# An eight-slot timetable for the way from attention into the feed-forward layer, and attention's scores in two PSUM banks

## What is computed

```python
x = layernorm(x + L0_attn(x))   # 16 heads of 16, q/k/v taken by a plain reshape, causal
x = layernorm(x + L0_ffn(x))    # router: 2 of 8 experts, gelu, all experts computed, gates applied
x = layernorm(x + L1_attn(x))   # 16 query heads of 128 in 4 groups
x = layernorm(x + L1_ffn(x))    # router with capacity 64 per expert
```

## Time and profile before

| what | value |
|---|---|
| median of 3 runs | 963.41 us (960.01 to 964.97) |
| the profiled execution: its own time, its span | 958.42 us, 956.6 us |
| TensorE busy | 862.1 us, 90% of the span |
| VectorE, ScalarE, GpSimd busy | 707.6, 513.9, 388.8 us |
| mean granted TensorE clock | 0.973 |

### The profile page before, as it was taken

How to read it: one execution, slowest core, us unless ns; L and a number is a source line. 1 busy time by engine, 2 the same in 40 slices (tenths; PEclk the granted TensorE clock), 3 DMA queues, 4 the chain that set the end, 5 groups by cost and what they waited for, 6 DMA issues and landing times.

```text
span 956.6 us, 22584 instructions
## 1 busy us (share of the span) xinstructions
PE 862.1 (90%) x8457; PEld 536.4 (56%) x8457; DVE 707.6 (74%) x1953; ACT 513.9 (54%) x1201; POOL 388.8 (41%) x731
## 2 busy tenths in 40 slices
PE   5899888987588888979999999999999999899996
PEld 2455444543344444445665766776676666587654
DVE  3776767676678787559999888888888888632566
ACT  3577667766234444446666555556555555523542
POOL 4445465534345645424343333333332323300285
PEclk7999999999789999999999999999999999999999
DMA  7333322320000000006576655565655655500011
GB/s 261 101 91 90 69 68 57 91 30 7 2 0 2 1 1 1 1 1 123 112 124 115 101 105 94 100 103 98 105 98 97 98 97 103 105 2 1 1 45 45
DMA packets 210428, 65.64 MB, mean 69 GB/s; under 512 B 203008, under 2 KB 206608, under 8 KB 210192
## 3 DMA queue, kind: packets, MB, share of 16 engines
q1 hardware_dynamic: 210320, 64.19, 33.8%
HBM read 17.92 MB, written 4.19 MB: 23 GB/s over the span
## 4 chain that ended last, share of the span: by engine, by line
PE 61%; DVE 12%; issue 10%; POOL 8%; DMA 4%; ACT 3%; SPq 1%; POOLq 0%; DVEq 0%; ACTq 0%
PE bank L418 13%; PE bank L420 12%; PE bank L419 12%; PE bank L545 4%; DMA att<-w_lo 4%; PE bank L769 3%; PE bank L771 3%; PE bank L770 3%; PE bank L466 2%; DVE scr L1215 2%; POOL scr L1727 2%; POOL rstd L1743 2%; DVE w_lo L1265 2%; DVE nm L1241 2%; POOL scr L1732 2%
## 5 line engine op out<-in xcount | busy, mean ns | idle before, releaser
L994 ACT ACTIVATE att<-att,nm 128x512 f32<-128x512 f32 (+3 forms) x256 | 141.5, 553 | 103.7 <-DVE nm L1254 102.3
L418 PE MATMUL bank<-w_hi,scr 128*128 128x256 bf16 (+1 forms) x576 | 173.5, 301 | 13.4 <-DVE scr L1183 12.9
L419 PE MATMUL bank<-w_lo,scr 128*128 128x256 bf16 (+1 forms) x576 | 173.1, 301 | 0.0
L420 PE MATMUL bank<-w_hi,scr 128*128 128x256 bf16 (+1 forms) x576 | 172.9, 300 | 0.0
L904 ACT ACTIVATE scr<-bank 128x256 bf16<-128x256 f32 (+3 forms) x208 | 110.8, 550 | 103.2 <-PE bank L771 41.2
L1241 DVE TENSOR_REDUCE nm<-bank 128x1 f32<-128x512 f32 (+3 forms) x256 | 110.3, 482 | 44.6 <-PE bank L490 42.8
L1254 DVE CUSTOM_DVE_ANT_0 att<-bank,consts 128x512 f32<-128x512 f32 (+3 forms) x256 | 113.3, 483 | 15.0 <-PE bank L420 15.0
L950 ACT ACTIVATE att<-bank 128x512 f32<-128x512 f32 (+1 forms) x192 | 90.9, 529 | 59.8 <-PE bank L529 59.1
L1775 POOL TENSOR_SCALAR wqkv_hi<-att,rr 128x512 bf16<-128x512 f32 (+3 forms) x128 | 65.6, 532 | 138.5 <-DVE rr L1271 138.5
L1775 POOL TENSOR_SCALAR w_hi<-att,rr 128x512 bf16<-128x512 f32 (+3 forms) x128 | 65.6, 532 | 106.5 <-DVE rr L1271 106.5
L1183 DVE TENSOR_TENSOR scr<-bank,scr 128x256 bf16<-128x256 f32 (+1 forms) x144 | 75.8, 536 | 43.1 <-ACT scr L904 43.0
(11 more groups left out here) (180 smaller groups left out, 2038.5 us busy)
## 6 DMA issues: line engine op xcount, KB each, us to landing
scr<-wall_in SPq DMA_DIRECT2D x19, 512.0 KB, 4.9
x_tok<-x_tok_in SPq DMA_DIRECT2D x1, 2048.0 KB, 10.5
v_by_token<-scr SPq DMA_DIRECT2D x16, 128.0 KB, 1.8
scr<-v_by_token SPq DMA_DIRECT2D x16, 128.0 KB, 3.2
scr<-x_t_in SPq DMA_DIRECT2D x3, 512.0 KB, 5.8
out<-x_tok SPq DMA_DIRECT2D x3, 512.0 KB, 2.6
scr<-wqkv_in SPq DMA_DIRECT2D x2, 384.0 KB, 3.4
att<-w_hi SPq DMA_TRANSPOSE x32, 3.3
```

The source lines that it names most:

```text
L418: pe.matmul(out, l_hi, r_hi, start=start, stop=False, skip_group_check=check)
L419: pe.matmul(out, l_hi, r_lo, start=False, stop=False, skip_group_check=check)
L420: return pe.matmul(out, l_lo, r_hi, start=False, stop=stop, skip_group_check=check)
L994: last = act.activation(at, at, ACT.Exp, bias=nm[:, j % 2, qt:qt + 1], scale=-1.0, accum_out=rs[:, j % 2, qt:qt + 1])
```

## The change

- Scores go to banks 0 and 1 alone; head h has bank h, and the hold is one head nearer: `- 1` for `- 2`.
- The V projection and the row of maxima move from bank 7 to bank 2. `l0_values` no longer waits for the K stack's copy but for the copy of the last maxima row (`qt`) and of the last V (`vt`); `l0_row_maxima` waits for `qt`, `vt` and, near the end, for the residual additions `r1` that read bank 2. `l0_stack` drops its waits for `qt` and `vt` and waits for the stack before.
- The steps n = -7 to -1 (seven instead of five) are taken apart and their pieces stand one by one in a table over slots 26 to 33 (`EARLY_AT`); `EARLY` now ends at 0, so that the mixture's step 0 follows slot 33 at once, and the first batch's `logits`, `route`, `choose` and `gate` are in the table too.
- The first six `turn_mix` (`LONE_TURNS`) use bank 7, each after the low part of the one before (`hold(pe, m["tlo"], i)`), and wait for the stacks' copies; the K stack of the last group waits for the two turns before it.
- GpSimd's and ScalarE's loops follow the same table; GpSimd's `add_bias` keeps its place at the ends of slots 27 to 30.
- No arithmetic is added or dropped.

```diff
@@ -67,11 +67,30 @@
-EARLY = range(-LEAD - 2, -2)
-TURNS = [(kind, n + lead) for n in STEPS for kind, lead in TURN_LEADS if 0 <= n + lead < NT]
+EARLY = range(-LEAD - 2, 0)
...
-EARLY_TURNS = sum(0 <= n + lead < NT for n in EARLY for _, lead in TURN_LEADS)
-EARLY_AT = {(NP - 2, 1): 0, (NP - 2, 2): 1, (NP - 1, 0): 2, (NP - 1, 1): 3, (NP - 1, 2): 4}
+EARLY_AT = {
+    (26, 1): (("context", 0),), (26, 2): (("cc", 0),),
+    (27, 0): (("cc", 1),), (27, 2): (("first", 0),),
+    (28, 0): (("join", 0), ("cc", 2)), (28, 1): (("norm", 0),), (28, 2): (("x1", 0), ("first", 1)),
+    (29, 0): (("join", 1), ("cc", 3)), (29, 1): (("norm", 1),), (29, 2): (("x1", 1), ("first", 2)),
+    (30, 0): (("join", 2), ("cc", 4)), (30, 1): (("norm", 2), ("first", 3)),
+    (30, 2): (("join", 3), ("x1", 2), ("cc", 5)),
+    (31, 0): (("norm", 3), ("first", 4)), (31, 1): (("x1", 3), ("join", 4), ("cc", 6)),
+    (31, 2): (("norm", 4), ("logits", 0)),
+    (32, 0): (("x1", 4), ("route", 0)), (32, 1): (("first", 5),), (32, 2): (("join", 5),),
+    (33, 0): (("choose", 0),), (33, 1): (("norm", 5),)}
+def early(p, chunk):
+    return EARLY_AT.get((p, chunk), ())
+TURNS = [(what, t) for at in sorted(EARLY_AT) for what, t in EARLY_AT[at] if what in ("cc", "x1")]
+TURNS += [(kind, n + lead) for n in STEPS[len(EARLY):] for kind, lead in TURN_LEADS if 0 <= n + lead < NT]
+LONE_TURNS = sum(what in ("cc", "x1") for at in EARLY_AT if at < (30, 0) for what, _ in EARLY_AT[at])
+FIRSTS = [at for at in sorted(EARLY_AT) for what, _ in EARLY_AT[at] if what == "first"]
...
@@ -308,7 +327,7 @@
         def turn_bank(i):
-            return i % 2
+            return 7 if i < LONE_TURNS else i % 2
...
@@ -438,9 +457,10 @@
             def l0_values(g):
...
-                hold(pe, a["stk"], g)
+                hold(pe, a["qt"], 2 * g - 3)
+                hold(pe, a["vt"], g)
...
-                    last = mm3(bank[7][:, 0:E], hi, lo, wqkv_hi[:, k, 512:768], wqkv_lo[:, k, 512:768],
+                    last = mm3(bank[2][:, 0:E], hi, lo, wqkv_hi[:, k, 512:768], wqkv_lo[:, k, 512:768],
...
@@ -450,9 +470,10 @@
             def l0_stack(g, which):
...
-                hold(pe, a["qt"], 2 * g - 2 + which)
+                hold(pe, m["tlo"], sum(what in ("cc", "x1") for at in EARLY_AT if at < (2 * g - 4 + which, 1)
+                                       for what, _ in EARLY_AT[at]))
...
-                    pe.wait_ge(a["vt"], g + 1)
+                    hold(pe, a["stk"], g)
...
@@ -474,13 +495,13 @@
-                out = [bank[(6 * p + 2 * chunk + h) % 3] for h in range(2)]
+                out = [bank[h] for h in range(2)]
...
-                                hold(pe, a["max"], 6 * p + 2 * chunk + h - 2)
+                                hold(pe, a["max"], 6 * p + 2 * chunk + h - 1)
...
@@ -496,16 +517,14 @@
             def l0_row_maxima(p):
...
-                if j == 1:
-                    pe.wait_ge(a["vt"], min(g + 3, NT))
-                    pe.wait_ge(a["stk"], min(g + 2, NT))
-                else:
-                    pe.wait_ge(a["stq"], min(g + 2, NT))
+                hold(pe, a["qt"], p)
+                hold(pe, m["r1"], sum(at < (p - 1, 0) for at in FIRSTS))
+                pe.wait_ge(a["vt"], min((p - 3) // 2 + 4, NT))
...
-                pe.matmul(bank[7][:, :], ident_b[:, :], q_stack[g % 2][:, ds(j * TOK, TOK)], start=True, stop=False,
+                pe.matmul(bank[2][:, :], ident_b[:, :], q_stack[g % 2][:, ds(j * TOK, TOK)], start=True, stop=False,
...
-                    last = pe.matmul(bank[7][:, qt * P:(qt + 1) * P], m_cols[p % 2][:, qt, :], ident_b[:, :],
+                    last = pe.matmul(bank[2][:, qt * P:(qt + 1) * P], m_cols[p % 2][:, qt, :], ident_b[:, :],
...
@@ -575,11 +594,21 @@
-                    if (p, chunk) in EARLY_AT:
-                        if EARLY_AT[p, chunk] == 0:
-                            pe.wait_ge(ch_done, 1)
-                            pe.wait_ge(a["max"], 6 * NP)
-                        early_step(EARLY[EARLY_AT[p, chunk]])
+                    for what, t in early(p, chunk):
+                        if what in ("cc", "x1"):
+                            if p < 30:
+                                pe.wait_ge(a["stk"], NT if p > 27 else NT - 1)
+                                pe.wait_ge(a["stq"], NT)
+                            else:
+                                pe.wait_ge(a["max"], 6 * NP)
+                            turn_mix(what, t)
+                        elif what == "first":
+                            if t == 0:
+                                pe.wait_ge(ch_done, 1)
+                            pe.wait_ge(a["qt"], min(p + 2, NP))
+                            first_project(t)
+                        elif what == "logits":
+                            logits(t)
...
             def turn_mix(kind, t):
...
@@ -594,7 +623,7 @@
-                hold(pe, m["tlo"], i - 1)
+                hold(pe, m["tlo"], i if i < LONE_TURNS else i - 1)
...
@@ -973,11 +1001,11 @@
-                    if (p, chunk) in EARLY_AT:
-                        n = EARLY[EARLY_AT[p, chunk]]
-                        if 0 <= n + LEAD:
-                            turned_high("x1", n + LEAD)
-                        turned_high("cc", n + LEAD + 2)
+                    for what, t in early(p, chunk):
+                        if what in ("cc", "x1"):
+                            turned_high(what, t)
+                        elif what == "route":
+                            router_exp(m, 1, TT * NX)
...
@@ -1347,14 +1388,27 @@
-                    if (p, chunk) in EARLY_AT:
-                        n = EARLY[EARLY_AT[p, chunk]]
-                        if n == EARLY[0]:
+                    for what, t in early(p, chunk):
+                        if what == "context":
+                            dve.wait_ge(v_wr, 16 * NT)
...
-                            context(0)
-                        if 0 <= n + LEAD:
-                            norm(n + LEAD, 1)
-                        early_step(n)
+                            context(t)
+                        elif what == "cc":
+                            turned_low(what, t)
+                            context(t + 1)
+                        elif what == "x1":
+                            turned_low(what, t)
+                        elif what == "join":
+                            joined(t, 1)
+                        elif what == "norm":
+                            norm(t, 1)
+                        elif what == "route":
+                            dve.wait_ge(a["pv"], 3 * NT)
+                            route(t)
+                        elif what == "choose":
+                            choose_first(t)
+                            choose_second(t)
+                            gate(t)
...
@@ -1692,8 +1719,11 @@
-                    if (p, chunk) in EARLY_AT:
-                        mix_step(EARLY[EARLY_AT[p, chunk]])
+                    for what, t in early(p, chunk):
+                        if what == "join":
+                            scale_and_shift(t, 1)
+                        elif what == "x1":
+                            add_out_bias(t)
```

More of the change, by code:

```diff
@@ L941, in l0_query_maxima @@
                 act.wait_ge(a["nm"], p + 1)
-                copy(q_max[p % 2], bank[7][:, :]).then_inc(a["qt"], 1)
+                copy(q_max[p % 2], bank[2][:, :]).then_inc(a["qt"], 1)
             def l0_exponentials(p, chunk):
@@ L1240, in l0_maxima @@
                         w = (qt + 1) * P
-                        last = dve.tensor_reduce(nm0[:, p % 2, h, qt:qt + 1], bank[n % 3][:, col:col + w], AX.X,
+                        last = dve.tensor_reduce(nm0[:, p % 2, h, qt:qt + 1], bank[n % 2][:, col:col + w], AX.X,
                                                  ALU.max)
@@ L1327, in sums_inverse, with route, choose_first, choose_second @@
                 dve.wait_ge(m["rc"], half + 1)
-            def early_step(n):
-                if 0 <= n + LEAD:
-                    turned_low("x1", n + LEAD)
-                if 0 <= n + LEAD + 1:
-                    joined(n + LEAD + 1, 1)
-                turned_low("cc", n + LEAD + 2)
-                context(n + LEAD + 3)
+            def route(b):
+                dve.wait_ge(m["lg"], b + 1)
+                tiles_b = slice(b * TT, (b + 1) * TT)
+                dve.tensor_tensor(lg[:, tiles_b, :], bank[2][:, 0:TT * NX].rearrange("p (t x) -> p t x", x=NX),
+                                  rb_bc[:, :].unsqueeze(1).to_broadcast([P, TT, NX]), ALU.add).then_inc(m["lgc"], 1)
+                dve.wait_ge(m["lgc"], b + 1)
+                router_max(dve, chain, lg[:, tiles_b, :], TT, m["lgd"])
+            def choose_first(b):
+                router_first(dve, chain, TT, m["ex"], b + 1)
+            def choose_second(b):
+                router_second(dve, chain, TT)
+            def gate(b):
+                tiles_b = slice(b * TT, (b + 1) * TT)
+                row, wide, top = router_views(TT)
```

(31 more changed lines are left out.)

19 lines of the change are left out of this document (5 added, 14 removed).

## The result

| | before | after |
|---|---|---|
| median of 4 runs | 962.93 us (960.01 to 964.97) | 947.25 us (945.18 to 950.19) |
| the profiled execution, its span | 958.42, 956.6 us | 945.18, 943.4 us |
| mean granted TensorE clock | 0.973 | 0.973 |

The ratio is 0.9853 (95% interval 0.9822 to 0.9884): 1.5% faster, where 1.1% was forecast. Two later sets of runs of the same kernel gave 0.9852 (0.9827 to 0.9877) and 0.9888 (0.9868 to 0.9907). One execution of the kernel with both edits, further down, took 2996 us and is left out of its numbers.

What follows compares the result with a forecast made beforehand. TensorE, busy 90%, was taken as the bound, so gains come from its idle time or low clock. Attention -9.1 and timetable -1.4 gave -10.5 us: 948 against the profiled 958.4, 953 on the median's footing, range 946 to 961.

Steps and rivals of the forecast that it cites:

- The V projection's wait: Steady attention: the V projection no longer waits for VectorE's K-stack copy; -0.90 us in each of 13 pairs of slots.
- The bank cost: Steady attention: with two score banks, scores wait for one more reduction; +0.1 us in odd and +0.1 in even slots.
- Rival (b): Attention pairs: VectorE's reductions set the pace, +0.6 us per pair, 970 us in all; chance 0.06.
- The filling: First attention slots, pipeline filling: the removed 1.4 us wait and three or four bare stalls of 0.4 to 0.6 cancel, 0.
- The timetable: Slot 26 to first experts: slots 26 to 29 +11.3 us, the rest -12.7, sum -1.4; queues on VectorE and GpSimd return the gain.
- the walk: Slot-by-slot count from slot 26 to the first experts, each instruction starting when engine and releasers are ready, at full clock.
- The clock: First experts: low clock after the last stall as before, no difference; a fall from slot 30's stall would cost 1 to 2 us.
- rival (c): Slots 26 to 33: norms caught by GpSimd's big bias additions, 2.0 us each, 959 us in all; chance 0.12.
- (a): Attention: bank stalls eat the gain, -0.1 us per pair, 961 us in all; chance 0.12.
- (e): Attention pair stays at 13.40 us because something else, such as ScalarE's exponentials, takes over; 961 us; chance 0.05.
- Rival (d): Timetable better than walked: biases find GpSimd free, slots 29 and 30 lose 1 us each, not 4; 947 us; chance 0.13.

Runs made afterwards that it cites:

- both edits: Kernel after with attention biases of batches 0 to 3 added in slots 26 and 27, and norm(5) ahead of choose: 941.29 and 942.07 us, ratios 0.9797 and 0.9795.
- the banks alone: Kernel before with only the bank part of the change, turns, biases and early blocks left as they were: 950.44 us, ratio 0.9876.
- the nearer hold: Kernel before with three score banks kept, but each head's scores waiting for one reduction more: 965.47 us, ratio 1.0043.
- the wait put back: Kernel after with the V projection again waiting for the K stack's copy of the group before: 964.32 us, ratio 1.0013.
- the first profile: Kernel after, unchanged, its first profiled execution: 945.18 us, span 943.4 us.
- the second execution: Kernel after, unchanged, profiled a second time: span 949.8 us; its set of runs had a median of 949.61 us.
- the third execution: Kernel after, unchanged, profiled a third time: 60.9 us from the fifteenth K stack to the first gelu; its set of runs 950.88 us.

## Why the prediction was right, point by point

The forecast was 953 in 946 to 961; measured were 947.25, and 949.6 and 950.9 in the later sets, all inside and all faster than the forecast. By the medians of each set the kernel gained 15.7, 12.8 and 11.5 us, forecast 10.5. Its mechanism held: the V projection's wait is the gain, and the queues on GpSimd and VectorE take back most of the timetable's.

- **The V projection's wait**, -0.90 per pair: right. Put back alone it costs 1.03 per pair and measures 0.98, and it is all of the attention gain.
- **The bank cost**, +0.1 and +0.1 per pair: right or over-sized, by where it is taken. It is 0.06 in the banks alone (0.90 less 0.84), 0.11 in the nearer hold, and 0.19 beside the wait put back (13.60 against 13.41). The two terms together were forecast as -0.7 per pair and are -0.84. The stall at the odd slot is 0.37 us, not 0.6, and lies in the shadow of the old wait for low parts; the even slot shows none. The pair is 12.57 us, not 12.7. Rival (b) would have needed 0.90.
- **The filling**, 0: this step failed. It costs +2.1 us between the first two profiles (2.6 in the nearer hold); over all profiles of both kernels the third K stack comes 0.6 to 2.7 us later. The prediction walked a full slot, where copies and projections cover the hand-overs; in the filling slots, as I read it, they are missing: the masks wait eight times between 23 and 40 us, where before one did (1.43 us). How much of the 2.1 us is these waits and how much a lower clock (0.65 from 27 to 34 us, before 0.90) no run separates. Some of the waits in the profile after:

```profile
23.82 0.29 PE L506 MATMUL bank<-past,ident_b 64*128 64x128 bf16 x1 [1.54 <-DVE nm L1264]
24.42 0.28 PE L506 MATMUL bank<-past,scr 64*128 64x128 bf16 x2 [0.31 <-DVE nm L1264]
...
34.08 0.23 PE L506 MATMUL bank<-past,scr 64*128 64x128 bf16 x2 [0.44 <-DVE nm L1264]
35.64 0.21 PE L506 MATMUL bank<-past,ident_b 64*128 64x128 bf16 x1 [0.43 <-DVE nm L1264]
```

- These two errors cancel: the pairs gave about 11.0 us, forecast 9.1, and the filling took back 2.1, forecast 0. The sum for attention, -9.1, stands against -8.9 measured; that it fits so closely is luck.
- **The timetable**, -1.4: slots 26 to 29 take 31.7 us, walked 32.8; slot 27 7.6 (7.7), slot 28 8.75 (8.6), slot 29 9.3 (10.3), slot 30 7.4 (8.0), slot 31 5.3 (5.6), the rest 10.2 (11.0). Every stall that the walk named is in the trace, at its place and with its releaser: the split behind the bias twice (2.91 us in slot 30, walked 2.7), norm(5) behind choose (5.99, walked 6.6). The walk was a little too slow nearly everywhere, 2.9 us in sum (its slots from 30 on add up to 24.6, not 24.7). By the timed medians the timetable gave 0.8 us against the banks alone, nearer to the forecast than the first profile's -4.3 us; that was an execution in which the clock stayed up behind the stalls of slots 29 and 30 and no norm was caught.
- **The clock**, 0: right before the first experts (0.62 in the window 253.7 to 258.3, before 0.53). A fall in slot 29 or 30 was priced at 1 to 2 us. In the second execution it cost some 2.3 us, and it made norm(3) so late that the bias addition caught it, 1.8 us more. This link between the clock and rival (c) is what the prediction didn't see.
- **Rival (c)** did not happen in the first profile and the third, and happened once in the second: norm(3) took 2.44 us beside an addition of 2.54 us, at the 2 us more that were priced. The walk's point, that GpSimd waits for a turn just when norms run, holds by a margin of 0.6 us for norm(3) (239.53 against 240.16), and a lower clock ahead of it is enough to lose that. In the first profile the closest is a norm of 0.82 us instead of 0.41, beside GpSimd's small bias addition. VectorE, then GpSimd:

```profile
239.53 0.82 DVE L1341 TENSOR_SCALAR x_tok<-x_tok,mv,rstd 128x256 f32<-128x256 f32 x1
```

```profile
239.45 0.75 POOL L1779 TENSOR_TENSOR x_tok<-x_tok,outb_bc 128x256 f32<-128x256 f32 x1
```

  The Trainium skill, page "SBUF — State Buffer", section "SBUF: two separate sides", has VectorE and GpSimd take turns at a shared port pair. The trace agrees with that in these rows, in those of the second execution and in the earlier trace rows.
- **Rivals (a), (b), (e)** fell with the pair of 12.57 us. **Rival (d)** was half right: slots 29 and 30 are shorter than walked, but by 1.0 and 0.6 us, not by 3 each.

Thirteen timed executions of the kernel after are on record: five took 944.5 to 946.9 us and eight 948.7 to 951.6. The first and third profile are of the five, the second is of the eight. Whether norm(3) was caught in all of the eight isn't shown; the other ten have no profile. Also open is why one execution of the kernel after lets the clock fall behind the stall of slot 29 and another before it. No experiment set the clock's state there.

## What to carry to other kernels

When two producers share a PSUM bank, look for the one that makes the engine that bounds the kernel wait for the other's reader. Moving that one to another bank was worth more here (12 us net) than a bank of slack for the scores (4 us, most of it in the filling). Price a tighter hand-over in the filling of a pipeline separately: the work that hides it in the steady part may not be there yet. In a timetable written by hand, follow each long off-path instruction on the helper engines: a bias addition of 2.35 us and 4 us of small router instructions stood ahead of what TensorE waited for, and two edits of their order gained 9 us beside the 11.5 of the whole change, in the same set of runs. Ask of such an instruction also by how much it misses the others: one that passes a norm by 0.6 us in one execution caught it in another.

## What the runs showed of the hardware that was not expected

The same program went through the same stretch in 60.0, 64.1 and 60.9 us. Behind the stalls of 2 to 3 us in slots 29 and 30 the granted clock was 1.00 in one execution and 0.72 and 0.69 in another, whose instructions stand in the same order. It fell behind shorter stalls too: in slot 27, behind 1.1 to 1.5 us of idle time, it was 0.72 from 206 to 212 us in the third execution of the kernel after and in the kernel with both edits, and 1.00 in the first two. Of the 4.1 us between two executions about 1.8 are one norm of 2.44 us beside a bias addition of 2.54 us, which the other execution missed by 0.6 us. With both edits the clock is 1.00 in the windows 226 to 231 and 236 to 241, and the timed runs lie within 1.5 us (941.5 to 943.0) where those of the kernel after beside them spread over 4.7 (946.9 to 951.5). With four runs of each this only suggests that removing such stalls and meetings also makes the time steadier.
